# A finer order for VectorE's steps in the attention stage, and buffers of its own for the last sequence's results

## What is computed

```python
x = L0_attn_x                                              # (8, 512, 256)
x = x + layernorm(attention(layernorm(x)))                 # rotary positions, causal softmax
h = layernorm(x)
scores = sigmoid(h @ gate_w.T)
topk_idx = top 4 of (scores + gate_bias), inside the best 2 of 4 groups
cw = scores at topk_idx, normalised, times 2.5
y = einsum(silu(h @ Wg.T) * (h @ Wu.T), cw, Wd)            # over 16 experts
y = y + silu(h @ Ws_g.T) * (h @ Ws_u.T) @ Ws_d.T
x = x + layernorm(h + y)
```

## Time and profile before

| | |
|---|---|
| median of three runs | 1031.69 us |
| the profiled execution | 1031.85 us |
| its span, first to last instruction | 1030.0 us |
| TensorE busy | 830.4 us (81%) |
| VectorE busy | 654.9 us (64%) |
| ScalarE, GpSimd busy | 452.2 us (44%), 434.8 us (42%) |
| mean granted clock of TensorE | 0.901 |

### The profile page before, as it was taken

The page is one execution under the profiler, slowest core; times in us unless marked ns, Lnnn a source line. Parts: engine busy times, 40 slices in busy tenths (PEclk is TensorE's granted clock), DMA queues, the critical chain, the costliest instruction groups (busy, mean ns, idle before and its releaser), DMA issues.

```text
span 1030.0 us, 20612 instructions
## 1 busy us (share of the span) xinstructions
PE 830.4 (81%) x6580; PEld 610.5 (59%) x6580; DVE 654.9 (64%) x1906; ACT 452.2 (44%) x763; POOL 434.8 (42%) x416
## 2 busy tenths in 40 slices
PE   3449887896898798698796887799988999988763
PEld 3326454564565465466464555688877788777521
DVE  4375758687687787777777694554553333877543
ACT  2115544553544455363464555555444455444300
POOL 4431203115425425424522424467567655655610
PEclk9758989899898899898898898899999999998977
DMA  4475744334444443533559422354556667988663
GB/s 164 118 189 149 226 109 126 81 84 138 127 112 116 130 123 118 136 102 98 157 156 304 138 88 91 109 177 150 175 172 217 201 168 265 337 302 305 237 234 123
DMA packets 89175, 168.72 MB, mean 164 GB/s; under 512 B 14704, under 2 KB 56688, under 8 KB 88816
## 3 DMA queue, kind: packets, MB, share of 16 engines
q1 hardware_dynamic: 75248, 128.85, 43.7%
q0 software_dynamic: 13824, 38.55, 9.9%
HBM read 90.15 MB, written 76.68 MB: 162 GB/s over the span
## 4 chain that ended last, share of the span: by engine, by line
PE 27%; DVE 12%; DMA 6%; issue 5%; SPq 4%; POOL 3%; ACT 2%; DVEq 0%; ACTq 0%; POOLq 0%
PE ring L1480 7%; PE ring L1501 3%; DVE nmax L781 3%; DMA xg<-sorted_rows 2%; PE ring L1259 2%; DMA ykt<-expert_rows 2%; PE ring L1466 2%; PE ring L1261 2%; PE ring L1260 2%; POOL expert_rows L699 2%; PE ring L1380 2%; SPq L592 2%; PE ring L1337 1%; DMA expert_rows<-ys,dest 1%; SPq L593 1%
## 5 line engine op out<-in xcount | busy, mean ns | idle before, releaser
L1189 ACT ACTIVATE prob<-ring 128x1024 f32<-128x1024 f32 (+1 forms) x192 | 167.4, 880 | 208.1 <-PE ring L1328 207.8
L781 DVE TENSOR_REDUCE nmax<-ring 128x2 f32<-128x1024 f32 (+3 forms) x256 | 200.8, 818 | 43.5 <-PE ring L1310 41.6
L699 POOL DMA_INDIRECT expert_rows<-ys,dest x160 | 157.7, 985 | 96.9 <-ACT ys L1143 40.5
L691 POOL DMA_INDIRECT sorted_rows<-xr,idx_all x128 | 131.0, 1023 | 79.7 <-DVE xr L940 46.6
L1480 PE MATMUL ring<-we,xh 128*128 x640 | 155.1, 386 | 0.0
L1480 PEld LDWEIGHTS ring<-we,xh 128*128 128x128 f32 x640 | 118.3, 195 | 13.3
L1003 DVE SCALAR_TENSOR_TENSOR sl<-sl,got,ring 128x128 f32<-128x128 f32 x160 | 48.3, 344 | 104.1 <-ACT sl L1241 103.8
L1322 PE MATMUL ring<-maskt_b,halves_b 64*128 64x128 bf16 (+2 forms) x768 | 57.2, 229 | 63.6 <-DVE nmax L781 37.0
L669 POOL TENSOR_TENSOR rot<-rot 128x512 f32<-128x512 f32 x16 | 20.4, 1278 | 204.6 <-DVE rot L773 204.6
L1322 PEld LDWEIGHTS ring<-maskt_b,halves_b 64*128 64x128 bf16 x768 | 22.5, 96 | 133.2 <-DVE nmax L781 53.7
L1337 PE MATMUL ring<-prob,v_sb 128*32 128x512 f32 (+3 forms) x1024 | 97.9, 481 | 1.7 <-ACT prob L1189 1.7
(11 more groups left out here) (194 smaller groups left out, 1673.7 us busy)
## 6 DMA issues: line engine op xcount, KB each, us to landing
xg<-sorted_rows SPq DMA_DIRECT2D x160, 134.0 KB, 2.5
parts<-part SPq DMA_DIRECT2D x32, 512.0 KB, 5.8
ykt<-expert_rows SPq DMA_DIRECT2D x16, 1024.0 KB, 9.4
k_st<-parts SPq DMA_DIRECT2D x64, 128.0 KB, 3.6
q_st<-parts SPq DMA_DIRECT2D x64, 128.0 KB, 3.5
we<-w_exp SPq DMA_DIRECT2D x1, 6144.0 KB, 21.9
sorted_rows<-zeros SPq DMA_DIRECT2D x2, 2144.0 KB, 12.0
sorted_rows<-zeros SPq DMA_DIRECT2D x32, 134.0 KB
```

The costliest lines, as they stand in the source:

```text
L691: pool.indirect_dma_start(out=xs[group_of(s)], out_offset=bass.IndirectOffsetOnAxis(ap=idx_all[:, s, t, k:k + 1], axis=0), in_=xr[:, s % 2 ...
L699: pool.indirect_dma_start(out=yk, out_offset=bass.IndirectOffsetOnAxis(ap=dest[:, j % 8, b:b + 1], axis=0), in_=ys[:, j % NYS, b, :], in_o ...
L781: dve.tensor_reduce(nmax[:, Q % 2, :, pp, qb], slot[:, :, col:col + (qb + 1) * P], AX.X, ALU.max, negate=True).then_inc(s_max, 1)
L1189: act_e.activation(prob[:, u % 2, 2 * half:2 * half + 2, 0:width], slot[:, :, 0:width], ACT.Exp, scale=SCALE).then_inc(s_exp, 1)
```

## The change

First, several steps of the plan are cut into pieces with numbers of their own: `LN` in three, `LNR` in two, `QK` in two (`QK`, `QKB`), `LNA` in three, `LNB` in seven, `LNC` in two, `Z` in two, `DP` in four, `GE` in four. All instructions of VectorE in a piece are those of before, with one exception: the residual sum `x1 + pr` is two instructions of half the size, not one. Second, the numbers of nearly all steps around them change. Third, sequence 7 has tiles of its own for results, in memory that the weights and activations of the first stage leave free, and all loads of the last group stand in the plan ahead of its sums. Each half's results are still one transfer of 1 MB.

```diff
-BEFORE = [("LX", -25), ("LN", -20.9), ("LNR", -19.2), ("XT", -16), ("QK", 0, -14.6), ("SPL", 0, -13.6), ("SPS", 0, -12.9),
-          ("QK", 1, -12.8), ("SPL", 1, -11.4), ("SPS", 1, -10.6), ("V", -5)]
-AFTER = [("X1L", 18), ("AT", 22), ("OP", 23), ("LNA", 24), ("LNB", 25.25), ("LNC", 26), ("HT", 27),
-         ("GU", 0, 28), ("GU", 1, 28.01), ("GA", 0, 28.5), ("GA", 1, 28.9), ("LG", 29.1)]
+BEFORE = [("LX", -25.7), ("LN", 0, -19.3), ("LN", 1, -19.05), ("LN", 2, -18.75), ("LNR", 0, -18.05), ("LNR", 1, -17.4),
+          ("XT", -16), ("QK", 0, -15.35), ("QKB", 0, -15.1), ("SPL", 0, -14.3), ("SPS", 0, -13.6),
+          ("QK", 1, -13.35), ("QKB", 1, -13.1), ("SPL", 1, -12.2), ("SPS", 1, -11.4), ("V", -5)]
+AFTER = [("X1L", 18), ("AT", 22), ("OP", 23), ("HT", 27.4),
+         ("GU", 0, 28.2), ("GU", 1, 28.21), ("GA", 0, 28.7), ("GA", 1, 29.0), ("LG", 29.1)]
...
+AFTER += [("LNA", i, (23.9, 24.25, 24.5)[i]) for i in range(3)]
+AFTER += [("LNB", i, (24.7, 24.75, 24.95, 25.25, 25.7, 25.95, 26.25)[i]) for i in range(7)]
+AFTER += [("LNC", i, (26.7, 26.95)[i]) for i in range(2)]
...
+AFTER += [("DP", i, (34.25, 34.5, 34.7, 34.95)[i]) for i in range(4)]
...
+    if end == B:
+
+        steps = [("CZ", g, s) for s in range(first, end)] + [("CL", g, *half) for half in halves]
+        for i, (s, h) in enumerate(halves):
+            steps += [("CA", g, s, h), ("CS", g, s, h)]
+            if i:
+                steps.append(("CN", g, *halves[i - 1]))
+        return steps + [("CN", g, *halves[-1])]
...
+        cursor[0] = w_low
+        ykt_last = place("ykt_last", [P, NT, TOPK, D])
+        zt_last = place("zt_last", [P, NT, D])
+        x1t_last = place("x1t_last", [P, NT, D])
...
+        def home(s):
+
+            return 2 if s == B - 1 else s % 2
+
+        def turn(s):
+
+            return 1 if s == B - 1 else s // 2 + 1
...
             def load_residuals(s):
-                if s >= 2:
-                    sp.wait_ge(s_out[s % 2], 32 * (s // 2))
+                _, z_home, x1_home = back(s)
+                if turn(s) > 1:
+                    sp.wait_ge(s_out[home(s)], 32 * (turn(s) - 1))
...
-                if s >= 2:
+                if turn(s) > 1:
                     sp.wait_ge(s_cn, N_OUT * (2 * (s - 2) + h + 1))
```

More of the change, by code:

```diff
@@ L210 @@
 N_STAT = 2 * NT + 1
-N_LN = 5 * NT + 1
+N_LN = 5 * NT + 2
 ROUTE_STEPS = 30
@@ L459, in block_kernel @@
         s_ysc = [sem(f"block_scattered{i}") for i in range(NYS)]
-        s_cl = [sem(f"parts_back{i}") for i in range(4)]
-        s_cz = [sem(f"residuals_back{i}") for i in range(2)]
+        s_cl = [sem(f"parts_back{i}") for i in range(6)]
+        s_cz = [sem(f"residuals_back{i}") for i in range(3)]
         s_cp = sem("results_summed")
@@ L467, in block_kernel @@
         s_cn = sem("final_rows")
-        s_out = [sem(f"out_stored{i}") for i in range(2)]
+        s_out = [sem(f"out_stored{i}") for i in range(3)]
         RELEASE = {
@@ L617, in store_out @@
                 tiles = slice(NHALF * h, NHALF * h + NHALF)
-                sp.dma_start(rows(out[s])[:, tiles, :], zt[:, s % 2, tiles, :]).then_inc(s_out[s % 2], 16)
+                sp.dma_start(rows(out[s])[:, tiles, :], back(s)[1][:, tiles, :]).then_inc(s_out[home(s)], 16)
             load_x(0)
@@ L655, in _ @@
                     store_out(st[2], st[3])
-            for par in range(2):
-                sp.wait_ge(s_out[par], 32 * (B // 2))
+            for place_of in range(3):
+                sp.wait_ge(s_out[place_of], 32 * max(turn(s) for s in range(B) if home(s) == place_of))
         @block.gpsimd
@@ L721, in _ @@
                     parts_low(n, st[2])
-                elif kind in ("LNA", "LNB"):
-                    post_rstd(n, int(kind == "LNB"))
+                elif kind == "LNA" and st[2] == 2:
+                    post_rstd(n, 0)
+                elif kind == "LNB" and st[2] == 6:
+                    post_rstd(n, 1)
                 elif kind == "GA":
@@ L760, in xt_low, with rotary @@
                     dve.tensor_tensor(xt_lo[:, k, :], slot[:, k, :], xt_hi[:, k, :], ALU.subtract).then_inc(s_xtlo, 1)
-            def rotary(s, qk, slot):
-                if s == 0 and qk == 0:
-                    dve.wait_ge(s_rope, 16)
-                if s or qk:
-                    dve.wait_ge(s_plo, 4 * s + 2 * qk)
+            def rotary(s, qk, slot, second):
                 cos, sin = rope_t[:, 0, :], rope_t[:, 1, :]
                 even, odd = slot[:, 0, :], slot[:, 1, :]
-                dve.wait_ge(s_qk, 4 * s + 2 * qk + 1)
-                dve.tensor_tensor(rot[:, 0, :], even, cos, ALU.mult).then_inc(s_rot, 1)
-                dve.tensor_tensor(rot[:, 2, :], even, sin, ALU.mult).then_inc(s_rot, 1)
+                if not second:
+                    if s == 0 and qk == 0:
+                        dve.wait_ge(s_rope, 16)
+                    if s or qk:
+                        dve.wait_ge(s_plo, 4 * s + 2 * qk)
+                    dve.wait_ge(s_qk, 4 * s + 2 * qk + 1)
+                    dve.tensor_tensor(rot[:, 0, :], even, cos, ALU.mult).then_inc(s_rot, 1)
+                    dve.tensor_tensor(rot[:, 2, :], even, sin, ALU.mult).then_inc(s_rot, 1)
+                    return
                 dve.wait_ge(s_qk, 4 * s + 2 * qk + 2)
@@ L799, in h_low, with statistics @@
                     dve.tensor_tensor(h_lo[:, k, :], slot[:, k, :], h_hi[:, k, :], ALU.subtract).then_inc(low_sem, 1)
-            def statistics(src, step, first, st, mv, ve, v_sem):
-                for t in range(NT):
-                    dve.bn_stats(st[:, t, :], src[:, t, :]).then_inc(step, 1)
+            def statistics(src, step, first, i):
+                if i < 2:
+                    for t in (2 * i, 2 * i + 1):
+                        dve.bn_stats(st2[:, t, :], src[:, t, :]).then_inc(step, 1)
+                    return
                 for t in range(NT):
```

154 lines of the change are left out of this document (92 added, 62 removed).

## The result

The changed kernel takes 1060.9 us, the median of 4 runs (1058.5 to 1064.3), beside 1032.0 for the kernel before on the same chip: 1.028 of before, 95% interval 1.0245 to 1.0316. It is 29 us slower; I had forecast 37 us less. The profiled execution took 1058.46 us, with a span of 1056.7 against 1030.0.

What follows compares the result with a forecast made beforehand. TensorE bounds the expert blocks; in the attention stage no engine is full and TensorE waits mostly for VectorE. Gains 10 + 8 + 8.9 + 3 + 9 less 3 make 36 us: 1031.85 to 996, called 995, range 970 to 1023.

Steps and rivals of the forecast that it cites:

- New costs: Attention stage: rotary steps hold one of three PSUM slots amid score units; 3 us lost, bounds 0 and 47.
- the fourth rival: Attention stage: scores wait behind the projection and its slot, 3.93 us for each of 12 steps; slower, 1040 us; chance 0.09.
- Term E: Tail: result loads issued together start the last sum 10.1 us earlier, less 1 for delayed scatters; 9 us gained.
- A: Attention stage: `DP` goes behind `AT` in pieces, so `h_lo` comes first; 10 us gained, bounds 0 and 12.1.
- B: Attention stage: `LN`'s statistics go behind `GU`'s products, ending four waits of 1.99 us; 8 us gained.
- C: Attention stage, `LNB`: its row operations no longer meet `SPL` on GpSimd, in sequences 1 to 4; 8.9 us gained.
- a period of 74 to 75 us: Attention stage, sign that the forecast is right: one sequence takes some 74 to 75 us, down from 80.
- under 2: Attention stage, sign that the forecast is right: `LNB`'s four row operations take under 2 us in all sequences.
- Term D: Table step `GE`: in four pieces with maxima between, it shortens `OP`'s 5.14 us wait; 3 us gained.
- The second rival: Attention stage: `SPL` meets other operations, and `weq<-weq,cw` waits for both GpSimd additions, 2.56 us; 1010 us; chance 0.14.
- The first rival: More than the sum: fewer stalls also give back TensorE's clock and half of the unbooked waits; 978 us; chance 0.15.

Runs made afterwards that it cites:

- e3_glued: The changed kernel with the pieces of the rotary steps and of the gate put back together, first chip: 1027.5 us, 0.9967 of before.
- e13_change: The changed kernel as it is, timed again on the fourth chip: 1090.6 us, 1.0048 of before.
- e14_together: The changed kernel with the pieces of the rotary steps and of the gate together, on the fourth chip: 1063.4 us, 0.9786 of before.
- e9_apart: Before's order with the new tail, and only the pieces of the rotary steps and of the gate set apart, third chip: 1.0063 of before.
- e4_qkback: The changed kernel with rotary steps, score layout, stores and gate wholly at before's numbers, first chip: 1031.5 us, 0.9994 of before.
- e12_dp: Before's order with the new tail, and only the dispatch moved, in four pieces behind `AT`, third chip: 0.9805 of before.

## Why the prediction was wrong

**The step that failed is the term "New costs", "Bounds: 0 and 12 steps x 3.93 = 47. I take 3".** It came to some 28 to 33 us. In the trace the rotary steps cost 14.6 + 9.9 = 24.5 us in 12 waits, 2.0 a step, not 3 for all of them, and the gate, which the term did not hold, 11.0 (before 0.7). Half of the mechanism, the slot that a rotary step holds, stood in the text as the fourth rival, with 0.09 and 1040 us, and even that was 21 us too low; the other half, the split, stood nowhere. I took the low end "since the steps of before stood among score units too, one of each pair directly". They did, but whole. I looked at where a step stands, not at whether anything stands between its pieces. The change had split the products that free the slot from those before them, and put a maximum that needs TensorE's next unit in between. That was to be read from the order: `L827` between `L816` and `L819`, with its `S` matmuls behind the projection. A slot of three was then held through a wait for TensorE itself. `e3_glued` and `e13_change` against `e14_together` show the cost from one side, `e9_apart` from the other, with waits for `rot` of 1.6 us at most where the change has up to 2.6. Its own cost is not known well enough to say whether the cut is dearer in the change's order.

**What the cut does not explain.** With the pieces together the kernel still took 1027.5 us, some 32 above the forecast. Its trace, against that of before, on the first chip: 10.6 us lost by the seventh quad, 18.4 gained up to the twenty-seventh (the forecast booked 30 for the first stage), 1.9 lost up to the first block pair, 10.8 lost from there to pair 10, 4.7 gained up to pair 20 and 0.2 in the rest of the blocks, 9.3 gained in the tail. By the last expert block nothing is left of the gain (its copy `ys` starts at 976.59 us in both traces), and the tail is the whole difference of the spans (1020.7 against 1030.0). So the sum also failed in two places that it did not hold, the start and the first expert blocks, and by some 12 us in the first stage.

**The start was not in the sum at all.** My stretch was 100 to 600 us; the first seven quads lost 18.0 us. With the pieces together 10.6 are left, so 7.4 belong to the pieces, and 10.6 to the early rotary steps of sequences 0 to 2: with these at before's numbers the seventh `o_t` comes at before's time (187.09), which was worth 0.008 on the fourth chip, hardly clear of the noise. In the changed kernel SyncE waits in order for the projected parts at the head of its queue (first row), then TensorE waits for the stacks:

```profile
56.03 10.91 SPq L560 DMA_DIRECT2D parts<-part  x4
```

```profile
77.23 0.79 PE L1371 MATMUL ring<-k_st,q_st 48*128 48x512 f32 x2 [8.81 <-DMA q_st<-parts]
```

**Term E, the tail, was right**: forecast 10.1 less 1, measured 10.2 in the trace and 0.008 (9 us) alone. The last blocks' scatter took 6.02 us, 6.08 in the earlier trace rows, so the residual loads cost nothing that shows.

**Terms A, B and C moved the waits that they named, but their sum is not confirmed.** I forecast a period of 74 to 75 us. With the pieces together it is 75.0 on the first chip, against 80.6. But of these 5.6 us 3.4 came with the early rotary steps: with them at before's places (`e4_qkback`) the period is 78.4. `h_lo` fell from 12.1 to 0.8 us (A); that the dispatch alone is worth its 10 us is where `e12_dp` points, and not shown. The waits for maxima ahead of projections (term B's, and most of 15.6) are down to 1.2, but 4.7 for `xt_lo` and 7.8 for `xr` came with the later `LN` and `LNC`. The row operations of `LNB` take 1.63 us for four, where I asked for under 2: the same operation took up to 2603 ns beside `SPL` and at most 482 where it does not meet it. It has one tensor and two scalars per row as inputs. The rule of the Trainium skill ("SBUF — State Buffer", "Who interferes with whom") that the prediction drew on speaks of two SBUF inputs, and fits `weq<-weq,cw`, which took 1.46 us beside `SPL` and 0.42 where it stands clear. What each of B and C gave by itself was not run.

**Term D, 3 us, is not settled.** `OP`'s wait of 5.14 us is gone, but the changed kernel waits 6.45 us for mask rows there, behind pieces of `GE` and of `LNA`:

```profile
590.19 0.34 PE L1390 MATMUL ring<-maskt_b,halves_b 64*128 64x64 bf16 x4 [6.45 <-DMA q_st<-mrow]
```

The second group's table, beside expert blocks, gained 4.7 us in the traces of the first chip (block pairs 10 to 20 took 35.6 us, before 40.3).

**The second rival** (the collision moves) was right that `weq<-weq,cw` would meet the additions, and wrong on the price: it took 1.12 us there, not 2.56, and 1.46 beside `SPL` before. With the pieces together it does not meet them at all.

**The first rival's** argument, that fewer stalls give back clock, has support. One window of 80 us hardly shows it (0.91 after, 0.90 before), three whole sequences do, before, after and with the pieces together (columns as in the earlier trace rows):

```profile
266.39:508.17 241.78, 200.61 (x1910) 139.05 (x1908) 182.07 (x454) 114.77 (x166) 99.59 (x89) 0.87 0.44 119
```

```profile
290.82:536.83 246.01, 197.88 (x1908) 136.39 (x1904) 176.43 (x456) 114.81 (x166) 95.84 (x87) 0.91 0.41 115
```

```profile
275.16:500.18 225.02, 193.12 (x1908) 130.31 (x1908) 180.72 (x458) 113.87 (x166) 95.42 (x87) 0.91 0.46 128
```

For the same matmuls TensorE is busy 200.6 - 193.1 = 7.5 us less with the pieces together, of the 16.8 us that the three sequences gained. Not all of it is clock, since the changed kernel, also at 0.91, is busy for 197.9. The time below the sum that the rival forecast did not come.

**Beside the first expert blocks** the changed kernel took 36.9 us from block pair 5 to 10 (starts of the copy `sl`, pairs counted from 0: 716.71 and 753.64), before 25.8; with the pieces together 36.6. The forecast booked nothing there. The variance of sequence 7 was ready at 725.40, but GpSimd computed its root 9.2 us later, behind a row of scatters that take 1.27 us each, and TensorE waited 6.58 us for the rows made from it (before, it waited 0.98):

```profile
733.62 0.96 POOL L730 DMA_INDIRECT sorted_rows<-xr,idx_all  x1 [0.30 <-issue]
734.60 1.04 POOL L720 TENSOR_TENSOR rstd<-ve,minus_half 128x4 f32<-128x4 f32 x1
```

```profile
737.90 0.66 PE L1341 MATMUL ring<-kc,xr 128*128 128x128 f32 x2 [6.58 <-DVE xr L886]
```

What that is worth in the end is not shown: on the other chips the wait was absent, or others stood in its place.

## What to carry to other kernels

Before a step is cut, ask what it holds until its last instruction, and whether something that stands between the pieces waits for the engine that is to get it back. Cut where nothing is held (a norm, a routing table: with these cut and the rotary steps whole at their old places a sequence took 2.2 us less here, 5.6 with the rotary steps early as well), and leave whole what frees a PSUM slot. A list of an engine's waits before the change prices what goes, not what comes: the new order must be read once for each resource with few slots, and the start and the end of the pipeline apart from its steady stage.

## What the runs showed of the hardware

The same kernel took 1032 us on one chip and 1087, 1102 and 1086 on three others. The mean granted clock was 0.896 on the first, and 0.879, 0.871 and 0.879 on those (medians of the kernel before). In the expert blocks TensorE was busy 231.4 of 250 us at 0.97 in the first trace (700 to 950 us), and 216.5 at 0.95 on the fourth chip (725 to 975 us), in before's order.

Not only the time but the ratio depends on the chip: the changed kernel was 1.028 of before on one and 1.005 on another, the version with the pieces together 0.997 and 0.979. With the pieces together the steady attention stage gained alike on both, 5.6 us a sequence on the first chip and 83.6 - 77.5 = 6.1 on the fourth. The traces part behind it: at the twenty-third `o_t` they are 8.0 and 8.8 us ahead of before's order, at the twenty-seventh 7.9 and 14.8. Why was not tested.
